# Self-attention: the region factor of three heads as three extra contraction rows of the scores, instead of a product and a sum on VectorE

## What is computed

```python
qkv = hidden_states @ c_attn_w + c_attn_b
q, k, v = jnp.split(qkv, 3, axis=-1)
scores = jnp.einsum('bhqd,bhkd->bhqk', q, k) / jnp.sqrt(jnp.float32(hd))
scores = jnp.where(causal[None, None], scores, mask_value)
attn = jax.nn.softmax(scores, axis=-1)
mult = _region_multipliers(S, H, FOCUS_FACTOR)   # heads 0, 1, 2: 1.6 on keys 0-84, 85-169, 170-255; else 1
scaled = attn * mult[None, :, None, :]
scaled = scaled / jnp.sum(scaled, axis=-1, keepdims=True)
attn = jnp.where(div_heads[None, :, None, None], scaled, attn)   # only heads 0, 1, 2
out = jnp.einsum('bhqk,bhkd->bhqd', attn, v)
```

## Time and profile before

| | us |
|---|---|
| median of 3 runs | 744.03 |
| lowest and highest | 739.29 and 744.41 |
| the profiled execution, its own time | 744.56 |
| its span on the core | 742.4 |
| outside the span | 2.16 |

### The profile page before, as it was taken

The page is one execution under the profiler, slowest core; times in us unless marked ns, Lnnn a source line. Parts: engine busy times, 40 slices in busy tenths (PEclk is TensorE's granted clock), DMA queues, the critical chain, the costliest instruction groups (busy, mean ns, idle before and its releaser), DMA issues. The chain is left out here.

```text
span 742.4 us, 10628 instructions
## 1 busy us (share of the span) xinstructions
PE 615.6 (83%) x3820; PEld 485.9 (65%) x3820; DVE 473.6 (64%) x770; ACT 300.4 (40%) x710; POOL 274.0 (37%) x166
## 2 busy tenths in 40 slices
PE   3998999999999899577777777876877458899898
PEld 2586899899899797434555556334444246677798
DVE  4287666766766533624788776599999982765400
ACT  1232454545454561033867733334444433543300
POOL 3035233332323300242755640247777774111000
PEclk9999999999999999878889989978999858999999
DMA  7014122121211000129980000000000524965000
GB/s 233 1 57 142 47 68 79 63 68 73 86 58 58 1 1 1 54 64 212 207 217 1 0 1 1 0 0 1 0 0 1 113 87 143 304 212 164 8 22 29
DMA packets 41561, 53.39 MB, mean 72 GB/s; under 512 B 3632, under 2 KB 37040, under 8 KB 41392
## 3 DMA queue, kind: packets, MB, share of 16 engines
q1 hardware_dynamic: 41520, 52.84, 25.1%
HBM read 48.63 MB, written 4.19 MB: 71 GB/s over the span
## 5 line engine op out<-in xcount | busy, mean ns | idle before, releaser
L187 POOL TENSOR_TENSOR ctx_lo<-ctx_stage,ctx_hi 128x1024 fp32r<-128x1024 f32 x32 | 77.2, 2416 | 159.7 <-DVE ctx_hi L470 159.7
L485 DVE TENSOR_TENSOR pT_lo<-ps,pT_hi 128x512 fp32r<-128x512 f32 x64 | 41.2, 685 | 60.8 <-ACT pT_hi L389 60.7
L284 PE MATMUL ps<-ctx_hi,pT_hi 128*128 128x256 f32 x256 | 75.0, 293 | 2.6 <-DVE pT_lo L485 2.6
L285 PE MATMUL ps<-ctx_lo,pT_hi 128*128 128x256 f32 x256 | 72.4, 283 | 0.0
L286 PE MATMUL ps<-ctx_hi,pT_lo 128*128 128x256 f32 x256 | 72.3, 283 | 0.0
L370 ACT CAST ctxT_hi<-ps 128x512 fp32r<-128x512 f32 x64 | 34.7, 592 | 78.1 <-PE ps L244 78.1
L1328 PE MATMUL pf<-phiT,disp 128*128 128x512 f32 x128 | 63.7, 621 | 0.0
L477 DVE TENSOR_SCALAR_CACHE_REDUCE scores<-ps,qbk 128x512 f32<-128x512 f32 x64 | 47.9, 749 | 19.6 <-PE ps L256 19.1
L1282 POOL TENSOR_TENSOR logits<-logits,cmax 128x2048 f32<-128x2048 f32 x8 | 41.4, 5181 | 45.3 <-DVE dwork L1498 45.3
L389 ACT CAST pT_hi<-ps 128x512 fp32r<-128x512 f32 x64 | 34.4, 591 | 42.5 <-PE ps L269 42.5
L380 ACT ACTIVATE probs<-scores,negmax 128x512 f32<-128x512 f32 x64 | 46.0, 729 | 13.5 <-DVE rowsum L496 13.5
(11 more groups left out here) (189 smaller groups left out, 1598.2 us busy)
## 6 DMA issues: line engine op xcount, KB each, us to landing
ctx_stage<-in_ctx_dram SPq DMA_DIRECT2D x32, 512.0 KB, 3.4
logits<-in_L_ffn_expert_w_dram SPq DMA_DIRECT2D x12, 1024.0 KB, 5.4
dwork<-in_L_ffn_expert_w_dram SPq DMA_DIRECT2D x4, 1024.0 KB, 6.2
qk_parts_dram<-qk_parts SPq DMA_DIRECT2D x8, 384.0 KB, 6.0
q_rows<-qk_parts_dram SPq DMA_DIRECT2D x24, 128.0 KB, 6.2
disp<-qk_parts_dram SPq DMA_DIRECT2D x24, 128.0 KB, 5.4
disp<-in_L_ffn_phi_w_dram SPq DMA_DIRECT2D x1, 2048.0 KB, 9.4
phiT<-in_L_ffn_expert_b_dram SPq DMA_DIRECT2D x4, 512.0 KB, 10.4
```

What stands on the lines that cost most here:

```text
L187: nc.gpsimd.tensor_tensor(ctx_lo[:, cols], ctx_in_sb[:, c % SLOTS, :], ctx_hi[:, cols].bitcast(F32), ALU.subtract).then_inc(split_g, 1)
L284: nc.tensor.matmul(pO[q][:, 0:D], pT_hi[:, c % 2, q, cols], hi, start=c == 0 and j == 0, stop=False)
L285: nc.tensor.matmul(pO[q][:, 0:D], pT_hi[:, c % 2, q, cols], lo, start=False, stop=False)
```

## The change

The factor is applied to the scores. ln 1.6 is written as the sum of three bf16 numbers (`focus_parts`). Each head of group 0 that has a region gets three more contraction rows behind its 96: in `q_rows` they hold 1, in `k_rows` they hold the three numbers for keys of the head's region and 0 elsewhere. The matmul with 99 rows then adds ln 1.6 to the scores of these keys, the row maxima and the exponentials take it in, and the row sums that ACT gives are the right ones. `stacked(head)` gives 99 rows for heads 0 to 2 and 96 for the others. Gone are the four DVE instructions of each focus unit and POOL's memsets of `focus`. New on DVE, ahead of the copies to `h2T`: a memset of ones in `q_rows`, a memset of zeros in `k_rows`, three small instructions that put the three numbers on three partitions, and three that add them to the regions of the keys.

```diff
+        def stacked(head):
+            return slice(0, ROWS + (NPART if head < FOCUSED else 0))
...
-            nc.gpsimd.memset(focus[:], 1.0).then_inc(const_g, 1)
...
-            nc.gpsimd.memset(focus[:, 0, 0:FIRST_END], FOCUS).then_inc(consts_g, 1)
-            nc.gpsimd.memset(focus[:, 1, FIRST_END:SECOND_END], FOCUS).then_inc(consts_g, 1)
-            nc.gpsimd.memset(focus[:, 2, SECOND_END:S], FOCUS).then_inc(consts_g, 1)
...
-                        nc.tensor.matmul(to[:, h * P:(h + 1) * P], q_rows[:, g * GH + h, first], k_rows[:, g * GH + h, first],
+                        rows = stacked(g * GH + h)
+                        nc.tensor.matmul(to[:, h * P:(h + 1) * P], q_rows[rows, g * GH + h, first], k_rows[rows, g * GH + h, first],
...
-            pe.wait_ge(consts_g, 5)
+            pe.wait_ge(consts_g, 2)
+            pe.wait_ge(frows_v, 5)
...
+            extra = slice(ROWS, ROWS + NPART)
+            nc.vector.memset(q_rows[extra, 0:FOCUSED, :], 1.0).then_inc(frows_v, 1)
+            nc.vector.memset(k_rows[extra, 0:FOCUSED, :], 0.0).then_inc(frows_v, 1)
+            for r, part in enumerate(focus_parts):
+                unit = ident[extra, ROWS + r:ROWS + r + 1]
+                if r:
+                    dve.wait_ge(focus_v, r)
+                    nc.vector.scalar_tensor_tensor(out=focus[extra, :], in0=unit, scalar=part, in1=focus[extra, :],
+                                                   op0=ALU.mult, op1=ALU.add).then_inc(focus_v, 1)
+                else:
+                    nc.vector.tensor_scalar(focus[extra, :], unit, part, None, ALU.mult).then_inc(focus_v, 1)
+            dve.wait_ge(focus_v, NPART)
+            dve.wait_ge(frows_v, 2)
+            for h, region in enumerate((slice(0, FIRST_END), slice(FIRST_END, SECOND_END), slice(SECOND_END, S))):
+                keys = k_rows[extra, h, :].rearrange("p (b s) -> p b s", b=B)[:, :, region]
+                nc.vector.tensor_scalar(keys, keys, focus[extra, 0:1], None, ALU.add).then_inc(frows_v, 1)
...
             def invert_sums(b, g, late):
                 G = NG * b + g
-                e = (eA, eB)[late]
                 first = late * GH
                 dve.wait_ge(exp_a, 2 * GH * G + (late + 1) * GH)
-                if g == 0:
-                    dve.wait_ge(consts_g, 5)
-                    nc.vector.tensor_tensor(e[:, 0, 0:3, :], e[:, 0, 0:3, :], focus[:, :, 0:(late + 1) * P], ALU.mult).then_inc(focus_v, 1)
-                    dve.wait_ge(focus_v, 2 * b + late + 1)
-                    nc.vector.reduce_sum(esum[:, 0, first:first + 3], e[:, 0, 0:3, :], axis=AX.X).then_inc(fsum_v, 1)
-                    dve.wait_ge(fsum_v, 2 * b + late + 1)
                 nc.vector.reciprocal(rinv[:, g, first:first + GH], esum[:, g, first:first + GH]).then_inc(rinv_v, 1)
```

More of the change, by code:

```diff
@@ L2 @@
+import math
 from contextlib import ExitStack
@@ L592, in self_attention @@
     SECOND_END = 2 * S // 3
-    FOCUS = 1.6
+    FOCUSED = 3
+    LOG_FOCUS = math.log(1.6)
     SCALE = HD ** -0.5
@@ L600, in self_attention @@
     STACK = len(Q_STACK)
+    ROWS = STACK * HD
     RING = 4
@@ L620, in self_attention @@
         rest = sb("qk_rest", [P, 2, HALF])
-        q_rows = sb("q_rows", [STACK * HD, NH, B * S], BF16)
+        q_rows = sb("q_rows", [ROWS + NPART, NH, B * S], BF16)
         v_all = sb("v_all", [P, TT, D])
@@ L625, in self_attention @@
         causal = sb("causal", [P, P], BF16)
-        focus = sb("focus", [P, 3, S])
+        focus = sb("focus", [P, 1])
         eA = sb("eA", [P, NG, GH, P])
@@ L664, in self_attention @@
         wq_a = sem("wq_a")
-        focus_v, fsum_v, rinv_v, norm_g = sem("focus_v"), sem("fsum_v"), sem("rinv2_v"), sem("norm_g")
+        focus_v, frows_v, rinv_v, norm_g = sem("focus_v"), sem("frows_v"), sem("rinv2_v"), sem("norm_g")
         t_mm, pT_a, pT_v, av_mm, o_a = sem("t2_mm"), sem("pT_a"), sem("pT_v"), sem("av_mm"), sem("o_a")
@@ L670, in self_attention @@
         phi_nat, phi_b_rest, free = phi_places(disp)
-        k_rows = free[0:STACK * HD, 0:NH * B * S // 2].bitcast(BF16).rearrange("p (h t) -> p h t", h=NH)
+        k_rows = free[0:ROWS + NPART, 0:NH * B * S // 2].bitcast(BF16).rearrange("p (h t) -> p h t", h=NH)
         W_IN = 16 * (4 + DH * HPH)
@@ L691, in qk_stage @@
             return QK_TILES[s % 4], slice(s // 4 * HALF, (s // 4 + 1) * HALF)
+        focus_parts = []
+        for _ in range(NPART):
+            left = LOG_FOCUS - sum(focus_parts)
+            step = 2.0 ** (math.frexp(left)[1] - 8)
+            focus_parts.append(round(left / step) * step)
         block = st.enter_context(nc.Block())
@@ L741, in _ @@
             nc.gpsimd.tensor_tensor(rstd[:], ve[:], power[:], ALU.pow).then_inc(rstd_g, 1)
-            pool.wait_ge(const_g, 3)
+            pool.wait_ge(const_g, 2)
             nc.gpsimd.affine_select(out=causal[:], in_=causal[:], compare_op=ALU.is_ge, fill=MASKED, base=0,
@@ L844, in score @@
                         head = g * GH + 2 * (part - 1) + i
-                        nc.tensor.matmul(to[:, i * S:(i + 1) * S], q_rows[:, head, bass.ds(b * S + P, P)],
-                                         k_rows[:, head, bass.ds(b * S, S)], start=i == 0, stop=False)
+                        rows = stacked(head)
+                        nc.tensor.matmul(to[:, i * S:(i + 1) * S], q_rows[rows, head, bass.ds(b * S + P, P)],
+                                         k_rows[rows, head, bass.ds(b * S, S)], start=i == 0, stop=False)
                     last = nc.tensor.matmul(to[:].rearrange("p (h k) -> p h k", h=2)[:, :, P:S], ident_bf[:],
```

## The result

The changed kernel takes 731.51 us (median of four runs, 730.16 to 731.94), the kernel before 741.68 on the same chip (four runs, 739.29 to 744.41). The ratio is 0.986, with a 95% interval of 0.981 to 0.991: faster by about 10.2 us. The profiled execution took 731.27 us.

The account below looks back on a forecast made before the run. In the loop a ring of DVE and ACT was taken as the bound, with no engine full. Terms -9.0 (loop), +0.3 (transfer), 0 (start) and 0 (PE) gave -8.7 us: 735.3 from the median 744.03, range 732.5 to 739.0.

Parts of the forecast that it names:

- the sum's best bound: Whole kernel: the largest gain allowed, -9.45 us, giving 734.6 us by the median.
- The loop: Self-attention loop: focus units of batches 1 to 3 become ordinary ones, gaining 3.15, 2.94 and 2.95 us, 9.04 in all.
- Batch 0's focus unit: First part of the self-attention: removing its product and sum only lengthens DVE's idle time waiting for ACT; gain 0.
- The transfer: Bias of the logits: its load lands 1.97 us earlier with the seventh store, leaving DVE a 0.3 us stall; bounds 0 and 2.3.
- The start: Start of the block: DVE's eight new instructions take 6.2 us, hidden before PE's first projection; cost 0, at worst 1.4 us.
- The cover: Start of the block: time by which DVE's copies end ahead of ACT's, which release PE's projection; 0.6 us.
- PE: Group 0's score matmuls: 99 contraction rows in place of 96 cost 0.
- should last as before: Sign to check: the part ahead of 308 us and the mixture of experts behind 453 us keep their length.
- A transfer that does not move: First rival: the bias still lands at 380.90, so the gain is 6.7 us, ending at 737.3; chance 0.18.
- The long unit: Second rival: a third engine keeps focus units midway between 7.4 and 4.5 us, ending at 739.9; chance 0.08.
- The lower clock: Third rival: PE stays at 1.2 GHz and bounds every unit at some 6 us, ending at 751; chance 0.03.
- Nothing: Fourth rival: DVE's time is hidden slack, leaving 744.0 plus at most 1.4 us of the start; chance 0.05.

Follow-up runs that it names:

- eB_kept: The changed kernel with only the second product and sum (on `eB`) put back on a tile of ones; 742.86 us, ratio to before 0.997.
- store_held: The changed kernel with SP's seventh store held back until ACT's 14th exponential instruction, going out at 359.37 instead of 358.02; 737.42 us, ratio to before 0.992.
- start_only: The changed kernel with DVE's product and sum put back for `eA` and `eB` on a tile of ones; 743.94 us, ratio to before 1.000.
- no_factor: The kernel before with DVE's product and sum of the focus units removed and nothing in their place; 732.42 us, ratio to before 0.988.
- b_dve_first: The kernel before with POOL's first dispatch product made to wait for DVE's; 741.93 us, ratio to before 1.001.
- the order forced: Both kernels with one engine's first dispatch product waiting for the other's: DVE first 733.15 after, 741.93 before; POOL first 733.83 after, 743.78 before.
- the two repeats: The changed kernel run again unaltered, beside the experiments: 731.41 us, ratio to before 0.988, and on another chip 733.15 us, ratio 0.986.

## Why the prediction was off

**What failed: the level that the gain was subtracted from, with a gain that was also counted too small.** The prediction takes its difference "from the median", 744.03 of three runs, and widens the range by what a median of few runs may be off. The three runs were 739.29, 744.03 and 744.41, so a middle value 2.4 us lower was as well supported as the one taken, and with one more run, 739.34, the median is 741.68. The level of this kernel is not sharp either way: beside the experiments it gave 741.29 (23 runs), 743.77 (29) and 744.62 (11), each on a chip of its own. From 741.68 the predicted -8.7 us ends at 733.0, inside the range; from 744.03 the measured -10.2 us ends at 733.9, inside it too. It took both misses. Of the 3.8 us by which the forecast missed, 2.35 are the level and 1.5 the sum. The range went 2.1 us below the sum's best bound (734.6 to 732.5), less than the level alone moved.

**The sum: -8.7 us, measured -10.2 (by other pairs -9.3 and -10.7).** The measured value lies beyond the sum's best bound, -9.45, but its interval, 7 to 14 us, holds both -8.7 and the -9.5 of the loop. Term by term:

- The loop, -9.04 predicted, measured -9.50. The mechanism stood in all three units, and `eB_kept` shows it for the second pair alone. The comparison was off: units alternate between about 4.49 and 4.26 us, and the focus units of batches 2 and 3 stand in the shorter place. Taking the 4.49 us unit next to them for what they would become cost 2 x 0.23 = 0.46 us. "The reciprocal of `eB` would then wait shortly for ACT" was a guess; in the focus units it does not wait but follows the copy directly (392.46 in the rows above). A pause of about 0.2 us stands in that place in the units of 4.49 us, and no row names what ends it.
- Batch 0's focus unit, 0 predicted. Right: 1.18 and 1.98 us more idle time.
- The transfer, +0.3 predicted, measured 0. The store moved by the 1.97 us forecast; the rest of the chain did not keep its length, as the prediction had assumed, but got 3.3 us shorter, 2.5 of them in the load of the bias. That was luck: no row had pointed to it. `store_held` shows that without the move the stall is 2.8 us.
- The start, 0 predicted, with 6.2 us for the eight instructions. Right: 5.2 us of work and 6.3 with gaps, ACT the releaser, and `start_only` at a ratio of 1.000. The value of 3.1 us for the ones was 0.5 too long, and 0.69 us ahead of them, which no term had, made that good. The cover is 0.9 us in place of 0.6 since ACT's copies end later: 13.97 us behind the load of `w_qkv`, before 13.62.
- PE, 0. Right by `start_only` and `no_factor`, and by the matmuls themselves: of the score matmuls of 256 columns in batches 1 and 2, the 6 with 99 rows and the 26 with 96 both have a mean of 276 ns.
- What the sum had no term for: the mixture of experts "should last as before" and was 3.95 us shorter. 2.9 of it are in the dispatch stretch (152.45 to 149.57), from the race, and 1.0 in the next piece (19.05 to 18.03), in which the granted clock is 0.90 of full speed after and 0.82 before. Neither needs the change: `b_dve_first`, with the old products and sums, has 149.74 and 18.03 us, and `store_held`, without them, 152.64 and 19.02 us. How much of the 10.2 us comes from here stays open; the medians with the order forced show none of it, and what the runs show is the loop's 9.5 us.

The windows of that next piece, before and then after, in the columns of the earlier trace rows, have nearly the same instructions in PE at the two granted clocks:

```profile
606.21:625.26 19.05, 15.61 (x72) 12.89 (x72) 6.53 (x13) 4.20 (x8) 13.63 (x5) 0.82 0.53 166
```

```profile
594.28:612.31 18.03, 14.71 (x73) 12.13 (x72) 6.57 (x13) 4.20 (x8) 13.47 (x5) 0.90 0.57 175
```

**The rivals.** A transfer that does not move did not happen; `store_held` puts its price at 2.8 us, against 2.3. The long unit did not show. The lower clock did not either: it was 1.00 over 380 to 400 us, 0.95 before. "Nothing" is out: the interval ends at 0.991.

**The chances.** Faster by over 1% had 0.62. It came out so, by 1.4% (1.2% and 1.4% in the two repeats), though the interval of the first pair and of one repeat reaches to 0.9%. The cut at 7.4 us stood close under -8.7, but each error in the sum could only be a stall that I had added or a gain that I had shaved; a range from 729 to 739 would have been what the spread of the runs asked for.

## What to carry to other kernels

An instruction of an in-order engine that stands in a ring behind the one wait of that ring costs its whole duration, and its removal gives it back whole, as the 3.15 us did in each of three units; what it will become is read from the unit in the same place of the period, not from its neighbour. When an engine gets faster, look at what it will ask for sooner, and at what it releases: here a load with 0.9 us to spare would have stopped the engine for 2.8 us (`store_held`), had the same change not sent its store off sooner. Before subtracting a gain from a median of three, look at the three: where they spread over 5 us, the time after is no better known than that, however well the gain is worked out, and the range has to be as wide downward as they are.

## What the runs showed that was not expected

- A DVE product of 128x768 with two inputs lasts 0.96 us alone, 1.15 when served ahead of POOL and 3.51 behind it; POOL's of 128x1280 lasts 2.35 us when served first and 3.11 behind DVE's. DVE's row started first by 0.34 us in the case in which it was served second. What decides it is open.
- A chain of stores and loads, one behind the other, from the seventh store to the landing of the bias took 18.4 or 22.2 us, depending on whether its first store went out at 358.0 or 359.4. So 1.35 us of delay became 5.1. Its last link, one load of 1024 KB, took 5.8 us and 8.5.
- Two memsets of three partitions each, 3072 elements of bf16 in 2.62 us and 1536 of uint32 in 1.34 us: 0.85 and 0.87 ns an element, less than the 1.0 ns taken in the prediction from DVE's products. Counted from the end of the instruction ahead of each (gaps of 0.69 and 0.27 us, for which the profile names no wait) they are 3.31 and 1.61 us, 1.08 and 1.05 ns an element.
- One kernel unchanged gave 736.70 to 746.83 us in 23 runs on one chip, and 736.70 to 747.70 over three. The changed kernel's 16 runs span 730.16 to 738.39. What makes the spread was not found.
